# A two-layer graph network on one core: masks moved between transpositions, and ten steps of rows loaded early into the tile of sums

## What is computed

```python
q = (h @ Wq + bq);  k = (k_edges @ Wk + bk);  v = (v_edges @ Wv + bv)   # 4 heads of 32
score = einsum('ehd,ehd->eh', q[dst], k) * scale
ex = exp(score - segment_max(score, dst)[dst])
attn = ex / segment_sum(ex, dst)[dst]
agg = segment_sum(v * attn, dst)
out = x + agg @ Wo + bo
```

## Time and profile before

| | before |
|---|---|
| median of three runs | 3288.93 us |
| the profiled execution | 3284.15 us, span 3282.4 us |
| TensorE busy (share of the span) | 2659.5 us (81%) |
| VectorE busy | 2409.7 us (73%) |
| ScalarE busy | 1868.0 us (57%) |
| GpSimd busy | 2122.8 us (65%) |
| mean rate of transfers | 229 GB/s |
| mean granted TensorE clock | 0.895 of 2.4 GHz |

### The profile page before, as it was taken

One profiled execution on the slowest core, in us unless ns is written; L12 is line 12 of the kernel. 1 busy time (PEld: TensorE's weight loads), 2 busy tenths in 40 slices (PEclk: granted clock), 3 DMA queues, 4 the chain that ended last, 5 costly groups with the idle time before them and its releaser, 6 DMA issues.

```text
span 3282.4 us, 63589 instructions
## 1 busy us (share of the span) xinstructions
PE 2659.5 (81%) x20446; PEld 1943.1 (59%) x20446; DVE 2409.7 (73%) x4642; ACT 1868.0 (57%) x6125; POOL 2122.8 (65%) x2014
## 2 busy tenths in 40 slices
PE   3446765988888887885670499999999999999988
PEld 2114442555555554553340388888888887888878
DVE  7799998999998888986960255555555556888876
ACT  0234447888887777873550255555555555666653
POOL 2388887888888888888877688888888881000000
PEclk9556666999999999997675799999999999999999
DMA  3255453555555555556896899999999997777751
GB/s 93 88 184 180 166 182 115 167 176 167 176 170 179 170 183 169 179 172 203 271 299 218 283 363 360 362 369 361 360 358 359 360 363 239 222 222 223 222 173 39
DMA packets 407231, 750.45 MB, mean 229 GB/s; under 512 B 47610, under 2 KB 283214, under 8 KB 406906
## 3 DMA queue, kind: packets, MB, share of 16 engines
q1 hardware_dynamic: 277866, 438.42, 42.0%
q0 software_dynamic: 96160, 291.60, 23.9%
q10 hardware_dynamic: 32880, 16.39, 1.7%
HBM read 500.16 MB, written 246.06 MB: 227 GB/s over the span
## 4 chain that ended last, share of the span: by engine, by line
PE 56%; POOL 19%; DVE 8%; issue 8%; ACT 4%; DMA 1%; DVEq 0%; POOLq 0%; SPq 0%; ACTq 0%
POOL table_s L575 18%; PE bank L1579 12%; PE bank L1606 12%; PE bank L1588 7%; PE bank L1597 6%; PE bank L1005 6%; PE bank L900 4%; PE bank L1573 3%; PE bank L986 3%; DVE parts L809 3%; ACT work L690 2%; PE bank L947 1%; POOL ring L563 1%; PE bank L1956 1%; DVE row_base L749 1%
## 5 line engine op out<-in xcount | busy, mean ns | idle before, releaser
L575 POOL DMA_INDIRECT table_s<-ring,place x1612 | 1854.8, 1151 | 481.5 <-issue 442.5
L651 ACT ACTIVATE row_base<-row_base 128x196 f32<-128x196 f32 x1414 | 495.8, 355 | 215.1 <-DVE row_base L745 215.1
L1682 DVE TENSOR_REDUCE gmax<-bank 128x1 f32<-128x384 f32 (+1 forms) x400 | 301.4, 753 | 279.8 <-PE bank L1579 270.4
L1641 ACT COPY exT<-bank 128x384 f32<-128x384 f32 x596 | 268.0, 483 | 404.6 <-PE bank L1597 400.7
L1579 PE MATMUL bank<-kT,G 128*128 128x512 f32 (+2 forms) x1192 | 472.9, 505 | 0.3 <-ACT kT L1634 0.3
L1606 PE MATMUL bank<-kv_rows,exT 128*128 128x129 f32 x3576 | 465.8, 275 | 0.1
L1634 ACT COPY kT<-bank 128x384 f32<-128x384 f32 x596 | 274.9, 485 | 288.0 <-PE bank L1588 286.3
L1606 PEld LDWEIGHTS bank<-kv_rows,exT 128*128 128x128 f32 x3576 | 431.5, 192 | 0.5 <-issue 0.5
L690 ACT CAST work<-bank 128x392 bf16<-128x392 f32 x784 | 353.5, 501 | 136.7 <-PE bank L986 125.0
L1005 PE MATMUL bank<-parts,work 128*128 128x384 bf16 x2401 | 429.6, 330 | 0.0
L1588 PE MATMUL bank<-ident,kv_rows 128*128 128x128 f32 x1788 | 298.2, 279 | 137.7 <-DMA kv_rows<-table_s 137.2
(11 more groups left out here) (301 smaller groups left out, 3944.8 us busy)
## 6 DMA issues: line engine op xcount, KB each, us to landing
kv_rows<-table_s SPq DMA_DIRECT2D x196, 816.0 KB
ring<-in_kv SPq DMA_DIRECT2D x278, 512.0 KB
kv_rows<-table_s SPq DMA_DIRECT2D x204, 408.0 KB, 4.0
ring<-in_kv POOLq DMA_DIRECT2D x124, 512.0 KB
table_s<-ring,place POOLq DMA_INDIRECT x1612
G<-G_dram SPq DMA_DIRECT2D x400, 64.0 KB
G_dram<-gst ACTq DMA_DIRECT2D x50, 256.0 KB, 4.4
x_dram<-xres ACTq DMA_DIRECT2D x5, 640.0 KB, 5.2
```

The lines of the kernel that those rows point to most:

```text
L575: pool.indirect_dma_start(out=m["table_s"], out_offset=bass.IndirectOffsetOnAxis(ap=m["place"][0:n, i, k:k + 1], axis=0), in_=m["ring"][0: ...
L651: last = nc.scalar.activation(at, at, ACT.Identity, accum_out=m["place_f"][:, i % 2, h * STREAMS // 2 + k:h * STREAMS // 2 + k + 1])
L1682: dve.tensor_reduce(gmax, of_scores(n), AX_X, ALU.max).then_inc(m["reduced"], 1)
```

## The change

Four things change. (1) In the first part `masks(n)`, with its two waits, leaves `score(n)` and is issued inside `keys(n)`, between its two groups of three transpositions; unit 0 and the extra and last units keep it in `score`. (2) The rows of steps 139 to 148 (`EARLY`) are loaded not into `ring` but into `early_rows`, a view of `agg` from column 3232 on (21760 numbers of each partition, tiles 25 to 193), from SP's queue, one behind each of the loads of steps 128 to 137. GpSimd's own loads begin with step 149 (`LATE`), issued in step 147. Before a sum is written over a step's rows, VectorE waits that the step has been sent. (3) Since `agg` lies over tiles of the nodes stage, SP waits at step 128 for all stores of G and of the residual (five waits that stood in front of layer 1's first load), and GpSimd waits for them ahead of step 136 and sets the unused columns of `early_rows` to one (a memset of 80 x 16 numbers in each partition). (4) In the output stage the bias is added ahead of `y`, and its semaphore is left out.

```diff
+EARLY = range(POOL_STEPS[1] + KRING, POOL_STEPS[1] + KRING + 10)
+EARLY_TILE = 25
+EARLY_TURN = 128
+EARLY_AT = -(-EARLY_TILE * VW // 16) * 16
+LATE = EARLY.stop
+def rows_of(m, i):
+    return m["early_rows"][:, i - EARLY.start, :, :] if i in EARLY else m["ring"][:, i % KRING, :, :]
@@ load_rows
-    need(eng, m["rows_sent"][u], sent_before(i))
+    ring = rows_of(m, i)
+    if i not in EARLY:
+        need(eng, m["rows_sent"][u], sent_before(i))
@@ scatter_rows
-    if i < LATE:
+    if i in EARLY:
+        pool.wait_ge(m["early_loaded"], 32 * len(EARLY))
+    elif i < LATE:
@@ nodes_stage, sync
         for i in range(POOL_STEPS[0] + KRING, POOL_STEPS[1] + KRING):
             load_rows(m, sp, i, m["rows_loaded"])
+            if i == EARLY_TURN:
+                for v in range(GSTS):
+                    sp.wait_ge(m["G_stored"][v], len(range(v, NT, GSTS)) * 16)
+                sp.wait_ge(m["x_stored"], NT // BATCH_T * 16)
+            if 0 <= i - EARLY_TURN < len(EARLY):
+                load_rows(m, sp, EARLY[i - EARLY_TURN], [m["early_loaded"]] * KRING)
@@ layer1_stage, sync: the same five waits are taken out
@@ layer1_stage, gpsimd
+        (the five waits)
+        pool.memset(m["early_rows"][:, :, :, ONE_AT:], 1.0).then_inc(m["ones_ready"], 1)
+        pool.wait_ge(m["ones_ready"], 2)
         for i in range(POOL_STEPS[1], STEPS):
             scatter_rows(m, pool, i, ("l1_summed", ROWS_EVERY, POOL_STEPS[1]))
-            if POOL_STEPS[1] < i < STEPS - KRING + 1:
+            if LATE - KRING < i < STEPS - KRING + 1:
@@ layer1_stage, tensor
         def score(n):
-            (waits and masks of n)
+            if n == 0 or unit(n)[0] != "first":
+                masks(n)
@@ keys(n), after the transpositions of group h
                 last.then_inc(m["turned"], 1)
+                if h == 0 and n > 0 and unit(n)[0] == "first":
+                    masks(n)
@@ layer1_stage, vector, add(n) of a first unit
+                for i in EARLY:
+                    if t == (EARLY_AT + (i - EARLY.start) * STREAMS * ROW) // VW:
+                        dve.wait_ge(m["rows_sent"][i % KRING], sent_before(i + KRING))
@@ output_stage, vector, own(i, u)
-            (need a_transposed; y; [x_reloaded]; bias, which counts bias_added)
+            ([x_reloaded]; bias; need a_transposed; y)
```

More of the change, by code:

```diff
@@ L120 @@
 SENT_BY = ((0, 0), (56, 38), (STEPS, 114))
-LATE = POOL_STEPS[1] + KRING
+EARLY = range(POOL_STEPS[1] + KRING, POOL_STEPS[1] + KRING + 10)
[3 more added lines that the diff above has]
+LATE = EARLY.stop
 KEY_RING = 3
@@ L132 @@
 SHIFT_STEPS = -(-(NT * PARTS + 4 * HEADS) // STREAMS)
+assert POOL_STEPS[0] + KRING <= EARLY_TURN <= POOL_STEPS[1] + KRING - len(EARLY)
 assert BATCH_T < X_OVERWRITTEN <= N // P and HC * (P + GW) <= X_OVERWRITTEN * D and SHIFT_STEPS <= POOL_STEPS[0]
@@ L549, in load_rows @@
             at, n = stream(first)
-            eng.dma_start(m["ring"][:, u, first:end, 0:2 * D], rows[:, at + i:at + i + (end - first - 1) * n + 1:n, :]).then_inc(loaded[u], 16)
+            eng.dma_start(ring[:, first:end, 0:2 * D], rows[:, at + i:at + i + (end - first - 1) * n + 1:n, :]).then_inc(loaded[u], 16)
     else:
         at, n = stream(SHORT)
-        eng.dma_start(m["ring"][:, u, SHORT:STREAMS - 1, 0:2 * D], rows[:, at + i:at + i + (STREAMS - SHORT - 2) * n + 1:n, :]).then_inc(loaded[u], 16)
-        eng.dma_start(m["ring"][0:TAIL, u, STREAMS - 1, 0:2 * D], m["kv"][P * W:E, :]).then_inc(loaded[u], 16)
+        eng.dma_start(ring[:, SHORT:STREAMS - 1, 0:2 * D], rows[:, at + i:at + i + (STREAMS - SHORT - 2) * n + 1:n, :]).then_inc(loaded[u], 16)
+        eng.dma_start(ring[0:TAIL, STREAMS - 1, 0:2 * D], m["kv"][P * W:E, :]).then_inc(loaded[u], 16)
 def scatter_rows(m, pool, i, paced):
@@ L562, in scatter_rows @@
         need(pool, m["rows_sent"][v], sent_before(j))
-        pool.tensor_copy(m["ring"][:, v, at:STREAMS, KEY_AT:KEY_AT + 1], m["sources"][:, j, at:STREAMS].rearrange("p (s a) -> p s a", a=1)).then_inc(m["keys_ready"], 1)
+        pool.tensor_copy(rows_of(m, j)[:, at:STREAMS, KEY_AT:KEY_AT + 1], m["sources"][:, j, at:STREAMS].rearrange("p (s a) -> p s a", a=1)).then_inc(m["keys_ready"], 1)
     pool.wait_ge(m["places_ready"], i + 1)
-    if i < LATE:
+    if i in EARLY:
+        pool.wait_ge(m["early_loaded"], 32 * len(EARLY))
+    elif i < LATE:
         pool.wait_ge(m["rows_loaded"][u], 32 * (i // KRING + 1))
     else:
-        pool.wait_ge(m["late_loaded"][u], 32 * ((i - LATE) // KRING + 1))
+        pool.wait_ge(m["late_loaded"][u], 32 * len(range(LATE + (u - LATE) % KRING, i + 1, KRING)))
     pool.wait_ge(m["keys_ready"], i + 1)
@@ L575, in scatter_rows @@
         pool.indirect_dma_start(out=m["table_s"], out_offset=bass.IndirectOffsetOnAxis(ap=m["place"][0:n, i, k:k + 1], axis=0),
-                                in_=m["ring"][0:n, u, k, :], in_offset=None).then_inc(m["rows_sent"][u], 16)
+                                in_=rows_of(m, i)[0:n, k, :], in_offset=None).then_inc(m["rows_sent"][u], 16)
 def scatter_stage(nc, m):
@@ L1537, in sync @@
             sp.wait_ge(m["rows_sent"][u], sent_before(FIRST_STEPS + (u - FIRST_STEPS) % KRING))
-        for v in range(GSTS):
-            sp.wait_ge(m["G_stored"][v], len(range(v, NT, GSTS)) * 16)
-        sp.wait_ge(m["x_stored"], NT // BATCH_T * 16)
         for n in range(UNITS):
@@ L1561, in gpsimd, with masks @@
     def gpsimd(pool):
+        for v in range(GSTS):
+            pool.wait_ge(m["G_stored"][v], len(range(v, NT, GSTS)) * 16)
+        pool.wait_ge(m["x_stored"], NT // BATCH_T * 16)
+        pool.memset(m["early_rows"][:, :, :, ONE_AT:], 1.0).then_inc(m["ones_ready"], 1)
+        pool.wait_ge(m["ones_ready"], 2)
         for i in range(POOL_STEPS[1], STEPS):
             scatter_rows(m, pool, i, ("l1_summed", ROWS_EVERY, POOL_STEPS[1]))
-            if POOL_STEPS[1] < i < STEPS - KRING + 1:
+            if LATE - KRING < i < STEPS - KRING + 1:
                 load_rows(m, pool, i + KRING - 1, m["late_loaded"])
     def tensor(pe):
+        def masks(n):
+            out = of_scores(n)
+            pe.wait_ge(m["l1_hot"], n + 1)
+            need(pe, m["exp_ready"], n - 1)
+            for j in range(unit(n)[2] * SGC):
+                pe.matmul(out[:, j * P:(j + 1) * P], m["others"][:, ring(n, OTHERS), j, :], m["out_b"][:, :], start=(j % 4 == 0), stop=False, skip_group_check=True)
         def score(n):
             out, wide = of_scores(n), unit(n)[2]
[L1570 to L1573, removed]
+            if n == 0 or unit(n)[0] != "first":
+                masks(n)
             pe.wait_ge(m["copied"], number["keys", n] + wide)
@@ L1913, in own @@
         def own(i, u):
-            need(dve, m["a_transposed"], i - 1)
-            dve.tensor_tensor(m["y"][:, u, :, :], m["agg"][:, bass.ds(i * PARTS, PARTS), 0:D],
-                              column(m["rl"][:, bass.ds(i * PARTS, PARTS)], [P, PARTS, D]), ALU.mult).then_inc(m["y_ready"], 1)
             if zero(i):
@@ L1920, in own @@
             dve.scalar_tensor_tensor(out=xr, in0=row_of(m["bvo"][:, :], [P, 1, D]), scalar=m["has"][:, bass.ds(i, 1)], in1=xr,
-                                     op0=ALU.mult, op1=ALU.add).then_inc(m["bias_added"], 1)
+                                     op0=ALU.mult, op1=ALU.add)
+            need(dve, m["a_transposed"], i - 1)
+            dve.tensor_tensor(m["y"][:, u, :, :], m["agg"][:, bass.ds(i * PARTS, PARTS), 0:D],
+                              column(m["rl"][:, bass.ds(i * PARTS, PARTS)], [P, PARTS, D]), ALU.mult).then_inc(m["y_ready"], 1)
             if not (isinstance(i, int) and i < 2):
@@ L1926, in add @@
             dve.wait_ge(m["o_summed"], i + 1)
-            dve.wait_ge(m["bias_added"], i + 1)
+            dve.wait_ge(m["y_ready"], i + 1)
             xr = m["x_again"][:, bass.ds(i, 1), :]
@@ L2030 @@
     decay_ready exp_ready l1_summed l1_added
-    xk_transposed xkT_ready xe_transposed xeT_ready y_ready a_transposed bias_added aT_ready o_summed o_added out_stored
+    xk_transposed xkT_ready xe_transposed xeT_ready y_ready a_transposed early_loaded aT_ready o_summed o_added out_stored
 """.split()
@@ L2186, in gnn_kernel @@
                 m[name] = place(back, name, shape, dt)
+            sums = m["agg"][:, :, :].rearrange("p t w -> p (t w)")
+            m["early_rows"] = sums[:, EARLY_AT:EARLY_AT + len(EARLY) * STREAMS * ROW].rearrange("p (i c w) -> p i c w", c=STREAMS, w=ROW)
             words = OTHERS * 2 * SGC * P // 2
```

## The result

The changed kernel takes 3249.77 us (median of four runs, 3246.82 to 3252.41) against 3288.97 (four runs, the three named above among them): ratio 0.9882, 95% interval 0.9867 to 0.9896. Faster by 39 us, inside the range, and 10 us more than forecast. The profiled execution took 3247.49 us with a span of 3245.6.

What follows compares the result with a forecast made beforehand. TensorE's chain was taken to bound layer 1's first part. Masks -35.1, five waits -0.2 and bias +6.2 sum to -29.1 us: 3255 us for an execution like the profiled one, 3260 us against the median; range 3248 to 3286.

Steps and rivals of the forecast that it cites:

- Masks: Layer 1's first part: masks between key transpositions close TensorE's gap, 0.18 us a unit, 35.1 us gained.
- I take no loss, since rows 2 show both changes of type without one: TensorE, first part: type changes around the moved masks cost nothing; up to 0.08 us a unit, 16 us, was possible.
- a gain beyond 0.20 us isn't possible: TensorE, first part: moving the masks saves at most the 0.20 us wait a unit; upper bound 40.6 us.
- Rival (d): TensorE, first part: masks don't fit the gap without loss, 0.08 us or more a unit; 3276 to 3285; chance 0.08.
- Early loads: Idle stretch before layer 1: ten steps loaded early cost 0, land before layer 1's first load, and relieve GpSimd.
- rival (e): Before layer 1: early loads slow the scatters by 10 us or more, delaying it; 3270 to 3289; chance 0.04.
- The 0.2 us for the five waits: SP's queue before layer 1's first load: moving five waits away saves 0.2 us, bounds 0 to 0.8.
- The seam: Change from first to second part: no new wait, cost 0; masks alone would leave it exposed by some 3 us.
- GpSimd: GpSimd's steps in the first part: 13.02 us, three units, instead of 13.56; last transfer at 2685 us.
- Rival (c): Change from first to second part: GpSimd's step stays 13.56 us, unit 196 waits about 19 us; 3279; chance 0.06.
- Transfers (a, b): First-part transfers: (a) 361 GB/s is top, 3285 us, chance 0.16; (b) rate sinks, 350 GB/s gives 3308, chance 0.07.
- Bias: Output stage: bias ahead of y adds 0.26 us a turn, 24 times, 6.2 us lost; bounds 0 and 8.4.

Runs made afterwards that it cites:

- e3: The kernel before with only the bias put ahead of y; 3296.40 us, ratio 1.0017 to the kernel before.
- e4: The kernel before with first-part masks moved behind the second three key transpositions, ahead of the sums, gap left; 3289.03 us, ratio 1.0000.
- e6: The changed kernel with y ahead of the bias again; 3248.47 us, ratio 0.9867 to the kernel before.
- e1: The kernel before with only the first-part masks moved between the key transpositions; 3248.97 us, ratio 0.9873.
- e10: The changed kernel with EARLY_TURN 126, y first, second-part masks between key transpositions and those of exponentials; 3258.33 us, ratio 0.9897 to the kernel before.
- e11: The kernel before with first-part masks directly behind the scores, ahead of the transpositions of exponentials, gap left; 3282.74 us, ratio 0.9975.
- e9: The changed kernel with EARLY_TURN 126, y first, second-part masks inside the three transpositions of exponentials; 3238.22 us, ratio 0.9837 to the kernel before.
- e2: The changed kernel with masks back in front of the scores and y ahead of the bias, so early loads alone; 3292.71 us, ratio 1.0007 to the kernel before.
- e12: The changed kernel, unaltered, measured again; 3253.14 us, ratio 0.9885 to the kernel before.
- e5: The changed kernel with EARLY_TURN 126 instead of 128, each early load two steps sooner; 3247.68 us, ratio 0.9875 to the kernel before.

## Why the prediction came out as it did

**Masks: right mechanism, size too small.** The gap of 0.18 us closed as worked out, and nothing came late in its place. The failed step is "I take no loss, since rows 2 show both changes of type without one". Rows 2 held a loss: the scores behind masks stood there with 1.35 us, and nothing in the trace of before showed them without it. I read the only example as the clean one. With no masks just ahead of them they take 1.29. So the term was 0.24 us a unit, 46.8 us, not 35.1; the first part shrank by 45.9. The bound "a gain beyond 0.20 us isn't possible" was wrong for the same reason: it bounded the wait, not the other side of the move. Rival (d), a loss between transpositions, didn't show: the loss lay at the masks' old place.

**Early loads: cost not nothing.** The failed step is "the last early load goes out behind turn 137, some 7 us before turn 138, so it is gone". It was issued at 1832.6, and with the load of step 137 just ahead of it step 135's last scatter landed late (5.78 us after its start, for 2.45): from last scatter to first row load 7.60 us for 4.25. That is rival (e) in small, 3.4 us of the 4.0 by which layer 1 began later; the rest is the spread of the earlier stages. The sign named for it, a first row load after 1842 us, did show, but it separates nothing: e3 and e4, without early loads, begin at 1847.8 and 1846.0. The length from the last scatter does. I had compared rates and not looked at the queue ahead of the one landing on which the path hangs. The 0.2 us for the five waits held (3.98 to 4.00 us at turn 126 for 4.25), and GpSimd's memset took 1.18 us and held nothing. The seam was right: some 3 us were forecast for it, 3.9 measured. At turn 128 cost and gain cancel (e6 against e1), so "they bring no time of their own" came true through a cost and a gain and not through nothing at either end.

**GpSimd.** Steps locked to three units (12.86 us at 4.28; 13.02 was worked out for 4.34), and the end came at 2683 us where 2685 was forecast. Rival (c) fell. Two readings behind this were too simple. Before, 13.56 us held for 34 of 40 steps between 2050 and 2600 us, with five of 12.3 to 13.0 among them, 13.45 on average; after, 41 of 42 take 12.82 to 12.87. And a transfer begun in VectorE's tile of masks doesn't last "until that is over": it ends some 0.84 us behind it.

**Transfers (a, b).** They gave 380 GB/s, and no wait for rows recurred. The step from "share 1.00 at 361 GB/s" to a top is what these rivals rested on; it doesn't hold. The figure of about 358 GB/s to a core's memory in the Trainium skill ("DMA: Bandwidth & Descriptors", Specifications) isn't a bound here either, by 590 us at 380.

**Bias.** 6.2 us were forecast; the turn grew by 0.18 us, not 0.26, since the bias starts sooner behind the sum than y did: sum to y was 0.60 us, and in the changed kernel, at 3192.77 to 3193.56 us, it is 0.52 to the bias and 0.27 from there to y. 24 x 0.18 = 4.3 us; the rest grew by 5.1, and e3 lost 5.6 us.

The sum with the measured terms: -46.8 + 4.0 + 5.1 = -37.7, for -36.8 in the span. The errors of 11.7 us (masks) and of 4.2 us (start, 4.0 for -0.2) went opposite ways. That the range held the time is luck in part: without the late landing the kernel would have come to about 3249.8 - 3.4 = 3246 us, under the lower end of 3248, which rested on the bound of 40.6 us for the masks.

## What to carry to other kernels

When an operation is moved on TensorE, cost both neighbours: the one it leaves and the one it now precedes. In this kernel the short masks cost 0.05 to 0.06 us in front of scores and sums and nothing in front of transpositions, and they were free inside a wait; so try each place and read the piece behind it. And before filling an idle stretch with transfers, look for the one landing that ends it and keep the queue empty for it.

## What was new about the hardware

- A block behind bf16 masks (56 ns each) took 0.05 to 0.06 us longer when its weight loads are of 192 ns (scores 1.35 for 1.29 and 0.70 for 0.65; sums 1.40 for 1.34 and 0.72 for 0.67), and 0.01 us or nothing when they are of 141 ns (transpositions: 0.33 for three in the changed kernel and 0.33 to 0.34 in e10, 0.66 for six in e11, 0.12 for one in e9). In all these runs long loads go with sums and scores and short ones with transpositions. Whether it is the length of the load that counts, or another difference between the two kinds, no run separates.
- A DMA share of 1.00 at 361 GB/s was not the top: the same mix went on to 380 GB/s, with a share of 1.01.
- From the start of a step's last scatter to the load that waits for its landing it took 2.45 us before and 4.9 to 5.8 us with 2 MB of loads queued 3.5 to 5.7 us ahead of that scatter (changed kernel, e2, e6, e12), though the mean rate of the stretch was only 305 GB/s. With the same early loads two steps sooner it was 2.44 us (e5).
- A GpSimd transfer begun while VectorE makes its tile of masks (0.96 us) ended some 0.84 us after VectorE was done (82 of them between 2050 and 2600 us in the changed kernel; 84 before, one of them 0.93), so it took up to 1.44 and 1.68 us; of the 506 begun outside it in the two traces three took more than 1.05 us, 1.06 at most.
